# Splitting the last 1024 rows of a graph layer (dropout, 8192 x 8192 by 8192 x 64 matmul, residual, layer norm) into 896 and 128

## The chip, the cores and the metric

The kernel runs on one core of a Trainium2 chip. The metric is the device time of one execution in microseconds. In the profile's names PE is TensorE (PEld its weight loads), DVE VectorE, ACT ScalarE, POOL GpSimd and SP SyncE; a q behind a name means that engine's own queue.

## What is computed

```python
def _L0_gnn_ref(x, adj, u):
    keep = (u >= 0.1).astype(x.dtype)
    x_drop = x * keep / (1.0 - 0.1)
    return jnp.matmul(adj, x_drop)

x = _layernorm(x + _L0_gnn_ref(x, adj, L0_gnn_u), axis=-1)   # (x - mean) / sqrt(var + 1e-5)
```

All is fp32: x and u are 8192 x 64 (2.1 MB each), adj is 8192 x 8192 (268 MB), the output is 8192 x 64. Each element of adj is used once for 64 columns of output.

## The kernel before

x is held as 128 partitions by 64 chunks (CHUNKS) by 64 columns (D). dropped holds the dropped-out and scaled x. The product is made transposed: a chunk of dropped (128 x 64) is the stationary operand, adj's transposed columns stream past it, and acc in PSUM collects the 64 output columns of 512 rows on 64 partitions. TILES = 2 such column tiles, at partitions 0 and 64, work on different rows, so a block is 1024 rows (BLOCK) and there are 8 blocks. The host has laid adj out so that a piece, 8 chunks of a block, is one contiguous 4 MB; a block has 8 pieces.

SP loads the pieces in order into four slots of raw (lines 88 to 97); it waits, for each slot, until PE has multiplied the piece that was in it (multiplied). The very last piece is loaded in four parts of 4, 2, 1 and 1 chunks (FINE, line 99), each with its own semaphore. PE waits for each piece and multiplies it (multiply, line 109): 16 matmuls of 512 columns, each shown as two records since the data are fp32, 32 in all. After a block, ACT copies acc into sums (take_sums, line 144), PE turns it back with four 128-column matmuls against an identity (turn, line 117), and DVE adds x (line 170), makes statistics of eight groups of 64 columns (174, 178), adds epsilon (181); POOL raises to the power of -0.5 (201), DVE normalises (187), and ACT issues the store (store, line 148). ACT runs this in the order take_sums, store for each block; each engine's program is a list in order, and nothing is reordered between the waits. For all blocks but the last, this lies beside the next block's loads.

Of the kernel before, what the change touches and what calls it, by code (L numbers as in the profile page):

```python
# [16 lines left out]
LAST = BLOCKS * PIECES - 1  # L17
SLOTS = 4
ROUNDS = PIECES // SLOTS
FINE = [(0, 4), (4, 6), (6, 7), (7, 8)]  # L20
DMA = 16
# [5 lines left out]
def dropout_matmul_layernorm(nc, x, u, adj, out):  # L27
# [7 lines left out]
    with ExitStack() as ctx:  # L35
# [11 lines left out]
        raw = sbuf("raw", [P, SLOTS, PER_PIECE, BLOCK])  # L47
        eye = sbuf("eye", [P, P])
        sums = sbuf("sums", [P, BANK])
# [30 lines left out]
        out_stored = semaphore("out_stored")  # L80

# [144 lines left out]
```

## Time and profile before

| | |
|---|---|
| median of 3 runs | 657.78 us |
| lowest, highest | 657.72, 659.25 us |
| the profiled execution | 659.25 us |
| its span, first to last instruction | 657.5 us |
| PE busy | 492.7 us, 75% |
| DMA, mean over the span | 418 GB/s |

The profile was taken on the execution that took 659.25 us. Its page gives busy times by engine, a picture of the span in 40 slices, the chain of work that ended last and groups of instructions; the timeline and the stretches (windows) can be asked for any part of the span. Times in them count from the span's start.

### The profile page before, as it was taken

Reading aid. Unit: us, or ns where it says so; the run is one execution under the profiler, and the core shown is the slowest. Engines: PE = TensorE matmul, PEld = TensorE weight load, DVE = VectorE, ACT = ScalarE, POOL = GpSimd, SP = SyncE. Lnnn points to the kernel's source line nnn. Section 1 sums busy time; section 2 is a strip of 40 time slices with the busy share of each in tenths; the row PEclk is TensorE's granted clock in tenths of the full one; section 3 lists DMA queues with packets and bytes.
Section 4 is the critical chain, followed back from the end, with each engine's and each line's share of the span. In section 5 each row is a group of like instructions: output and inputs, shape, how many; then the busy total and the mean of one; then the engine's idle time right before and its main releaser. Section 6 shows DMA issues by size and latency. Waiting matters only on the chain.

```text
span 657.5 us, 4821 instructions
## 1 busy us (share of the span) xinstructions
PE 492.7 (75%) x2112; PEld 156.1 (24%) x2112; DVE 42.7 (6%) x210; ACT 6.0 (1%) x9; POOL 13.9 (2%) x15
## 2 busy tenths in 40 slices
PE   0587787786887697686796687877787688868784
PEld 0122222221222222222232222322232122312221
DVE  3000002000020001100020000200002000110002
ACT  0000000000000000000000000000000000000000
POOL 0000001000000000000000000000000000000000
PEclk9997989998989998998999988998999988999888
DMA  9999999999999999999999999999999999999980
GB/s 375 425 442 419 443 426 434 431 435 429 437 429 429 437 425 441 431 425 437 435 427 431 439 425 437 427 433 437 429 435 427 436 431 437 425 431 436 429 358 16
DMA packets 11094, 274.81 MB, mean 418 GB/s; under 512 B 1232, under 2 KB 1232, under 8 KB 2512
## 3 DMA queue, kind: packets, MB, share of 16 engines
q1 hardware_dynamic: 9936, 272.63, 96.5%
q10 hardware_dynamic: 1152, 2.10, 0.8%
q8 instruction: 4, 0.07, 0.0%
q14 instruction: 2, 0.02, 0.0%
HBM read 272.63 MB, written 2.10 MB: 418 GB/s over the span
## 4 chain that ended last, share of the span: by engine, by line
DMA 68%; PE 18%; issue 12%; DVE 1%; another core or an unknown queue 1%; SPq 0%; POOLq 0%; POOL 0%; ACT 0%; DVEq 0%
DMA raw<-adj_dram 68%; PE acc L109 17%; POOLq L35 0%; DVE normed L187 0%; POOL rstd L201 0%; PE turned L117 0%; DVE stats L174 0%; SPq L89 0%; SPq L94 0%; DVE rows L170 0%; DVE moments L178 0%; ACT sums L144 0%; SPq L87 0%; SPq L86 0%
## 5 line engine op out<-in xcount | busy, mean ns | idle before, releaser
L109 PE MATMUL acc<-raw,dropped 128*64 128x512 f32 x2048 | 483.6, 628 | 150.4 <-DMA raw<-adj_dram 150.4
L109 PEld LDWEIGHTS acc<-raw,dropped 128*64 128x64 f32 x2048 | 148.4, 144 | 479.7 <-issue 279.7
L170 DVE TENSOR_TENSOR rows<-turned,x_sb 128x512 f32<-128x512 f32 x8 | 5.5, 692 | 586.3 <-PE turned L117 586.3
L201 POOL TENSOR_TENSOR rstd<-var_eps,minus_half 128x8 f32<-128x8 f32 x8 | 13.1, 1640 | 638.5 <-DVE var_eps L181 638.5
L187 DVE TENSOR_SCALAR normed<-rows,moments,rstd 128x64 f32<-128x64 f32 x64 | 15.0, 310 | 14.1 <-POOL rstd L201 14.1
L117 PE MATMUL turned<-eye,sums 128*128 128x128 f32 x64 | 9.3, 288 | 5.5 <-ACT sums L144 5.5
L117 PEld LDWEIGHTS turned<-eye,sums 128*128 128x128 f32 x64 | 7.7, 191 | 12.5 <-ACT sums L144 12.5
L144 ACT COPY sums<-acc 128x512 f32<-128x512 f32 x8 | 4.7, 586 | 640.6 <-PE acc L109 640.6
L174 DVE BATCH_NORM_STATS2 stats<-rows 128x6 f32<-128x64 f32 x64 | 8.9, 212 | 0.3
L178 DVE BATCH_NORM_AGGREGATE moments<-stats 128x2 f32<-128x6 f32 x64 | 5.1, 153 | 0.3
L163 DVE TENSOR_TENSOR dropped<-dropped,x_sb 128x4096 f32<-128x4096 f32 x1 | 4.4, 4426 | 2.7 <-DMA x_sb<-x_dram 2.7
L159 DVE TENSOR_SCALAR dropped<-dropped 128x4096 f32<-128x4096 f32 x1 | 2.3, 2294 | 8.5 <-DMA dropped<-u_dram 8.5
L181 DVE TENSOR_SCALAR var_eps<-moments 128x8 f32<-128x8 f32 x8 | 1.4, 172 | 0.3
L144 ACT ACT_TABLE_LOAD x1 | 1.3, 1283 | 0.7 <-PEq L219 0.7
L196 POOL TENSOR_SCALAR_AFFINE_SELECT eye<-eye 128x128 f32<-128x128 f32 x1 | 0.3, 295 | 0.2 <-POOL eye L194 0.2
L194 POOL MEMSET eye<- 128x128 f32 x1 | 0.2, 205 | 0.0
L193 POOL MEMSET minus_half<- 128x8 f32 x1 | 0.1, 105 | 0.3 <-POOLq L219 0.3
L219 POOL MEMSET const-float32-0.0<- 128x1 f32 x1 | 0.1, 99 | 0.2 <-issue 0.2
L219 POOL MEMSET const-bfloat16-1.0<- 128x1 bf16 x1 | 0.1, 102 | 0.0
L219 POOL MEMSET const-uint8-127<- 128x1 uint8 x1 | 0.1, 102 | 0.0
L219 POOL MEMSET const-float32-1.0<- 128x1 f32 x1 | 0.1, 99 | 0.0
## 6 DMA issues: line engine op xcount, KB each, us to landing
raw<-adj_dram SPq DMA_DIRECT2D x63, 4096.0 KB, 31.5
dropped<-u_dram SPq DMA_DIRECT2D x1, 2048.0 KB, 7.7
x_sb<-x_dram SPq DMA_DIRECT2D x1, 2048.0 KB, 12.2
out_dram<-normed ACTq DMA_DIRECT2D x8, 256.0 KB, 14.3
raw<-adj_dram SPq DMA_DIRECT2D x1, 2048.0 KB, 26.9
raw<-adj_dram SPq DMA_DIRECT2D x1, 1024.0 KB, 29.0
raw<-adj_dram SPq DMA_DIRECT2D x2, 512.0 KB, 30.1
```

Of the source, the lines that this page charges most:

```text
L109: last = nc.tensor.matmul(acc[t * D:(t + 1) * D, :], dropped[:, c, :], raw[:, i % SLOTS, j, t * BANK:(t + 1) * BANK], start=(c == 0), stop ...
L117: last = nc.tensor.matmul(turned[:, i * TILES:(i + 1) * TILES, :], sums[:, i * P:(i + 1) * P], eye[:, :], start=True, stop=True)
L144: nc.scalar.copy(sums[:, :], acc[:, :]).then_inc(sums_ready, 1)
L159: nc.vector.tensor_scalar(dropped[:, :, :], dropped[:, :, :], P_DROP, 1.0 / (1.0 - P_DROP), ALU.is_ge, ALU.mult).then_inc(drop_scaled, 1)
L163: nc.vector.tensor_tensor(dropped[:, :, :], dropped[:, :, :], x_sb[:, :, :], ALU.mult).then_inc(x_dropped, 1)
L170: nc.vector.tensor_tensor(rows[:, :, :], turned[:, :, :], x_sb[:, b * GROUP:(b + 1) * GROUP, :], ALU.add).then_inc(rows_ready, 1)
L174: last = nc.vector.bn_stats(stats[:, i, :], rows[:, i, :])
L178: last = nc.vector.bn_aggr(moments[:, i, :], stats[:, i, :])
L181: nc.vector.tensor_scalar(var_eps[:, :], moments[:, :, 1], EPS, None, ALU.add).then_inc(var_ready, 1)
L187: last = nc.vector.tensor_scalar(normed[:, i, :], rows[:, i, :], moments[:, i, 0:1], rstd[:, i:i + 1], ALU.subtract, ALU.mult)
L201: nc.gpsimd.tensor_tensor(rstd[:, :], var_eps[:, :], minus_half[:, :], ALU.pow).then_inc(rstd_ready, 1)
L219: nc = bacc.Bacc("TRN2", target_bir_lowering=False, num_devices=1)
```

## The change

The first seven blocks stay as they are. The last 1024 rows become two parts.

NEXT is 896 rows: 448 in each column tile, all 64 chunks, in loads of 8, 8, 8, 8, 8, 8, 7, 5 and 4 chunks from an array of its own, adj_next, in which a partition's row holds all 64 chunks (224 KB). Its seven groups are turned (turn_next: three full matmuls, and two half ones for the group whose two halves lie in different tiles), normalised and stored as a block is.

FINAL is the last 128 rows. Both column tiles work on the same rows, tile 0 on chunks 0 to 31 and tile 1 on chunks 32 to 63: 32 pairs (PAIRS) of 128-column matmuls into final_acc, from loads of 10, 8, 6, 4, 2 and 2 pairs out of adj_final into slot 0. The turn of NEXT stands on PE behind the first of them, followed by a matmul that puts x of the last group into final_turned. At the end ACT copies final_acc to final_sums, one matmul against join (two identities, one above the other) turns it and adds the two halves onto x in final_turned, and DVE makes statistics and normalises straight from PSUM, one group wide; POOL has one more power. SP stores the last group. In ACT's program the copy stands behind NEXT's store.

The diff, cut to its core (declarations of the new tiles and semaphores, and edits of the normalising helper that only replace GROUP by groups, are left out):

```diff
@@ -6,25 +6,35 @@
 N = 8192
 D = 64
 CHUNKS = N // P
-BANK = 512
 TILES = 2
-TURNS = BANK // P
-BLOCK = TILES * BANK
-BLOCKS = N // BLOCK
-GROUP = TURNS * TILES
+DMA = 16
+
+
+WIDTH = 512
+GROUP = 8
+BLOCKS = 7
 PER_PIECE = 8
 PIECES = CHUNKS // PER_PIECE
-LAST = BLOCKS * PIECES - 1
 SLOTS = 4
 ROUNDS = PIECES // SLOTS
-FINE = [(0, 4), (4, 6), (6, 7), (7, 8)]
-DMA = 16
+ROW = PER_PIECE * TILES * WIDTH
+
+
+NEXT_WIDTH = 448
+NEXT_GROUP = 7
+NEXT = [(0, 0, 8), (1, 8, 16), (2, 16, 24), (3, 24, 32), (0, 32, 40), (1, 40, 48), (2, 48, 55), (3, 55, 60),
+        (3, 60, 64)]
+NEXT_ROUND = [s for s, _, _ in NEXT].index(0, 1)
+
+
+PAIRS = CHUNKS // TILES
+FINAL = [(0, 10), (10, 18), (18, 24), (24, 28), (28, 30), (30, 32)]
 
 P_DROP = 0.1
 EPS = 1e-5
 
 
-def dropout_matmul_layernorm(nc, x, u, adj, out):
+def dropout_matmul_layernorm(nc, x, u, adj, adj_next, adj_final, out):
     fp32 = mybir.dt.float32
     ALU = mybir.AluOpType
 
...
@@ -86,72 +112,111 @@
-                sp.dma_start(raw[:, s, :, :], adj[s]).then_inc(raw_loaded[s], DMA)
-            rounds = BLOCKS * ROUNDS
-            with sp.Fori(1, rounds - 1) as g:
+                sp.dma_start(raw[:, s, :], adj[s]).then_inc(raw_loaded[s], DMA)
+            with sp.Fori(1, BLOCKS * ROUNDS) as g:
                 for s in range(SLOTS):
                     sp.wait_ge(multiplied, (g - 1) * SLOTS + s + 1)
-                    sp.dma_start(raw[:, s, :, :], adj[g * SLOTS + s]).then_inc(raw_loaded[s], DMA)
-            for s in range(SLOTS - 1):
-                sp.wait_ge(multiplied, (rounds - 2) * SLOTS + s + 1)
-                sp.dma_start(raw[:, s, :, :], adj[(rounds - 1) * SLOTS + s]).then_inc(raw_loaded[s], DMA)
-            sp.wait_ge(multiplied, LAST - SLOTS + 1)
-            for f, (c0, c1) in enumerate(FINE):
-                sp.dma_start(raw[:, SLOTS - 1, c0:c1, :],
-                             adj[LAST][:, c0 * BLOCK:c1 * BLOCK]).then_inc(fine_loaded[f], DMA)
+                    sp.dma_start(raw[:, s, :], adj[g * SLOTS + s]).then_inc(raw_loaded[s], DMA)
+            chunk = TILES * NEXT_WIDTH
+            for n, (s, c0, c1) in enumerate(NEXT):
+
+                first_in_slot = c0 if s != SLOTS - 1 or n < NEXT_ROUND else NEXT[-2][1]
+                at = (c0 - first_in_slot) * chunk
+                sp.wait_ge(multiplied, BLOCKS * PIECES - SLOTS + min(n, len(NEXT) - 2) + 1)
+                sp.dma_start(raw[:, s, at:at + (c1 - c0) * chunk],
+                             adj_next[:, c0 * chunk:c1 * chunk]).then_inc(next_loaded[n], DMA)
+
+            sp.wait_ge(multiplied, BLOCKS * PIECES + NEXT_ROUND + 1)
+            for n, (q0, q1) in enumerate(FINAL):
+                sp.dma_start(raw[:, 0, q0 * TILES * P:q1 * TILES * P],
+                             adj_final[:, q0 * TILES * P:q1 * TILES * P]).then_inc(final_loaded[n], DMA)
+            sp.wait_ge(normed_ready, BLOCKS + 2)
+            sp.dma_start(out_dram[:, (CHUNKS - 1) * D:], final_normed[:, :]).then_inc(final_stored, DMA)
+            sp.wait_ge(final_stored, DMA)
...
-            def multiply(i, c0, c1):
-                for j in range(c0, c1):
-                    c = i * PER_PIECE + j
+            def multiply(s, at, c0, c1, width):
+                for c in range(c0, c1):
                     for t in range(TILES):
-                        last = nc.tensor.matmul(acc[t * D:(t + 1) * D, :], dropped[:, c, :],
-                                                raw[:, i % SLOTS, j, t * BANK:(t + 1) * BANK],
+                        start = at + ((c - c0) * TILES + t) * width
+                        last = nc.tensor.matmul(acc[t * D:(t + 1) * D, 0:width], dropped[:, c, :],
+                                                raw[:, s, start:start + width],
                                                 start=(c == 0), stop=(c == CHUNKS - 1))
                 return last
 
-            def turn(b):
-                pe.wait_ge(sums_ready, b + 1)
-                for i in range(TURNS):
-                    last = nc.tensor.matmul(turned[:, i * TILES:(i + 1) * TILES, :],
-                                            sums[:, i * P:(i + 1) * P], eye[:, :], start=True, stop=True)
-                last.then_inc(block_turned, 1)
+            def multiply_final(q0, q1):
+                for q in range(q0, q1):
+                    for t in range(TILES):
+                        start = (q * TILES + t) * P
+                        last = nc.tensor.matmul(final_acc[t * D:(t + 1) * D, 0:P], dropped[:, t * PAIRS + q, :],
+                                                raw[:, 0, start:start + P],
+                                                start=(q == 0), stop=(q == PAIRS - 1))
+                return last
+
+            def turn(groups):
+                for i in range(groups // TILES):
+                    last = nc.tensor.matmul(turned[:, i * TILES:(i + 1) * TILES, :], sums[:, i * P:(i + 1) * P],
+                                            eye[:, :], start=True, stop=True)
+                return last
+
+            def turn_next():
+                turn(NEXT_GROUP)
+
+                for t in range(TILES):
+                    last = nc.tensor.matmul(turned[t * D:(t + 1) * D, NEXT_GROUP - 1, :],
+                                            sums[:, NEXT_WIDTH - D:NEXT_WIDTH], eye[:, t * D:(t + 1) * D],
+                                            start=True, stop=True)
+                return last
...
-            with pe.Fori(0, BLOCKS - 1) as b:
+            pe.wait_ge(join_ready, 1)
+            with pe.Fori(0, BLOCKS) as b:
                 for i in range(PIECES):
                     pe.wait_ge(raw_loaded[i % SLOTS], (b * ROUNDS + i // SLOTS + 1) * DMA)
-                    multiply(i, 0, PER_PIECE).then_inc(multiplied, 1)
-                turn(b)
-            for i in range(PIECES - 1):
-                pe.wait_ge(raw_loaded[i % SLOTS], ((BLOCKS - 1) * ROUNDS + i // SLOTS + 1) * DMA)
-                multiply(i, 0, PER_PIECE).then_inc(multiplied, 1)
-            for f, (c0, c1) in enumerate(FINE):
-                pe.wait_ge(fine_loaded[f], DMA)
-                last = multiply(PIECES - 1, c0, c1)
-            last.then_inc(multiplied, 1)
-            turn(BLOCKS - 1)
+                    multiply(i % SLOTS, 0, i * PER_PIECE, (i + 1) * PER_PIECE, WIDTH).then_inc(multiplied, 1)
+                pe.wait_ge(sums_ready, b + 1)
+                turn(GROUP).then_inc(block_turned, 1)
+            for n, (s, c0, c1) in enumerate(NEXT):
+                pe.wait_ge(next_loaded[n], DMA)
+                at = (c0 - NEXT[-2][1]) * TILES * NEXT_WIDTH if n == len(NEXT) - 1 else 0
+                multiply(s, at, c0, c1, NEXT_WIDTH).then_inc(multiplied, 1)
+            for n, (q0, q1) in enumerate(FINAL):
+                if n == 1:
+                    pe.wait_ge(sums_ready, BLOCKS + 1)
+                    turn_next().then_inc(block_turned, 1)
+
+                    nc.tensor.matmul(final_turned[:, 0:D], eye[:, :], x_sb[:, CHUNKS - 1, :], start=True, stop=False)
+                pe.wait_ge(final_loaded[n], DMA)
+                last = multiply_final(q0, q1)
+            last.then_inc(final_multiplied, 1)
+            pe.wait_ge(final_sums_ready, 1)
+            nc.tensor.matmul(final_turned[:, 0:D], final_sums[:, :], join[:, :],
+                             start=False, stop=True).then_inc(final_done, 1)
...
-            def take_sums(b):
-                act.wait_ge(multiplied, (b + 1) * PIECES)
+            def take_sums(b, done, width):
+                act.wait_ge(multiplied, done)
                 if b:
 
                     act.wait_ge(rows_ready, b)
-                nc.scalar.copy(sums[:, :], acc[:, :]).then_inc(sums_ready, 1)
-
-            def store(b):
+                nc.scalar.copy(sums[:, 0:width], acc[:, 0:width]).then_inc(sums_ready, 1)
+
+            def store(b, groups):
                 act.wait_ge(normed_ready, b + 1)
-                act.dma_start(out_dram[:, b * GROUP * D:(b + 1) * GROUP * D],
-                              normed[:, :, :]).then_inc(out_stored, DMA)
+                act.dma_start(out_dram[:, b * GROUP * D:(b * GROUP + groups) * D],
+                              normed[:, 0:groups, :]).then_inc(out_stored, DMA)
 
             for b in range(BLOCKS):
-                take_sums(b)
-                store(b)
-            act.wait_ge(out_stored, BLOCKS * DMA)
+                take_sums(b, (b + 1) * PIECES, WIDTH)
+                store(b, GROUP)
+            take_sums(BLOCKS, BLOCKS * PIECES + len(NEXT), NEXT_WIDTH)
+            store(BLOCKS, NEXT_GROUP)
+            act.wait_ge(final_multiplied, 1)
+            nc.scalar.copy(final_sums[:, :], final_acc[:, 0:P]).then_inc(final_sums_ready, 1)
+            act.wait_ge(out_stored, (BLOCKS + 1) * DMA)
...
+            for b in range(BLOCKS):
+                normalise(b, GROUP)
+            normalise(BLOCKS, NEXT_GROUP)
+
+            dve.wait_ge(final_done, 1)
+            nc.vector.bn_stats(final_stats[:, :], final_turned[:, 0:D]).then_inc(stats_ready, 1)
+            dve.wait_ge(stats_ready, BLOCKS + 2)
+            nc.vector.bn_aggr(final_moments[:, :], final_stats[:, :]).then_inc(moments_ready, 1)
+            dve.wait_ge(moments_ready, BLOCKS + 2)
+            nc.vector.tensor_scalar(final_var[:, :], final_moments[:, 1:2], EPS, None, ALU.add).then_inc(var_ready, 1)
+            dve.wait_ge(rstd_ready, BLOCKS + 2)
+            nc.vector.tensor_scalar(final_normed[:, :], final_turned[:, 0:D], final_moments[:, 0:1],
+                                    final_rstd[:, 0:1], ALU.subtract, ALU.mult).then_inc(normed_ready, 1)
...
-            nc.gpsimd.memset(eye[:, :], 0.0).then_inc(eye_zeroed, 1)
-            pool.wait_ge(eye_zeroed, 1)
+            nc.gpsimd.memset(eye[:, :], 0.0).then_inc(squares_zeroed, 1)
+            nc.gpsimd.memset(join[:, :], 0.0).then_inc(squares_zeroed, 1)
+            pool.wait_ge(squares_zeroed, 2)
             nc.gpsimd.affine_select(out=eye[:, :], in_=eye[:, :], compare_op=ALU.not_equal, fill=1.0,
                                     base=0, pattern=[[-1, P]], channel_multiplier=1).then_inc(eye_ready, 1)
+            nc.gpsimd.affine_select(out=join[:, :], in_=join[:, :], compare_op=ALU.not_equal, fill=1.0,
+                                    base=0, pattern=[[-1, D]], channel_multiplier=1).then_inc(join_half, 1)
+            pool.wait_ge(join_half, 1)
+            nc.gpsimd.affine_select(out=join[:, :], in_=join[:, :], compare_op=ALU.not_equal, fill=1.0,
+                                    base=-D, pattern=[[-1, D]], channel_multiplier=1).then_inc(join_ready, 1)
...
+            pool.wait_ge(var_ready, BLOCKS + 2)
+            nc.gpsimd.tensor_tensor(final_rstd[:, :], final_var[:, :], minus_half[:, 0:1],
+                                    ALU.pow).then_inc(rstd_ready, 1)
...
-    pieces = by_row.transpose(1, 5, 4, 6, 3, 2, 0)
+    by_group = np.asarray(adj).reshape(P, CHUNKS, P, CHUNKS).transpose(1, 2, 3, 0)
+
+    full = by_group[:BLOCKS * GROUP].reshape(BLOCKS, GROUP // TILES, TILES, P, PIECES, PER_PIECE, P)
+    full = full.transpose(0, 4, 3, 5, 2, 1, 6)
+
+    first = CHUNKS - 1 - NEXT_GROUP
+    whole = by_group[first:CHUNKS - 2].reshape(NEXT_GROUP // TILES, TILES, P, CHUNKS, P).transpose(2, 3, 1, 0, 4)
+    halves = by_group[CHUNKS - 2].reshape(P, CHUNKS, TILES, P // TILES)
+    nxt = np.concatenate([whole.reshape(P, CHUNKS, TILES, -1), halves], axis=3)
+
+    final = by_group[CHUNKS - 1].reshape(P, TILES, PAIRS, P).transpose(0, 2, 1, 3)
```

## Rows read from the trace of the kernel before

**Rows 1.** The page: span, DMA's busy tenths in 40 slices, HBM bytes

```profile
span 657.5 us, 4821 instructions
...
DMA  9999999999999999999999999999999999999980
...
HBM read 272.63 MB, written 2.10 MB: 418 GB/s over the span
```

**Rows 2.** A stretch of the middle: busy time of each engine, clock, DMA share, GB/s

```profile
core 0: us, PE busy (x) PEld busy (x) DVE busy (x) ACT busy (x) POOL busy (x), PEclk, DMA share, GB/s
100.00:200.00 100.00, 78.14 (x336) 25.16 (x336) 8.99 (x52) 0.86 (x2) 3.29 (x2) 0.95 1.00 432
```

**Rows 3.** The page's chain that ended last, by line

```profile
DMA raw<-adj_dram 68%; PE acc L109 17%; POOLq L35 0%; DVE normed L187 0%; POOL rstd L201 0%; PE turned L117 0%; DVE stats L174 0%; SPq L89 0%; SPq L94 0%; DVE rows L170 0%; DVE moments L178 0%; ACT sums L144 0%; SPq L87 0%; SPq L86 0%
```

**Rows 4.** Timeline of PE and its weight loads near the end: start, length, instructions [idle before]

```profile
601.91 0.20 PEld L109 LDWEIGHTS acc<-raw,dropped 128*64 128x64 f32 x4 [3.49 <-DMA raw<-adj_dram]
...
621.34 7.09 PE L109 MATMUL acc<-raw,dropped 128*64 128x512 f32 x32 [1.03 <-DMA raw<-adj_dram]
631.05 15.65 PE L109 MATMUL acc<-raw,dropped 128*64 128x512 f32 x64 [2.62 <-DMA raw<-adj_dram]
```

**Rows 5.** Stretches near the end (columns as in group 2)

```profile
632.00:634.00 2.00, 2.00 (x8) 0.69 (x6) 0.00 (x0) 0.00 (x0) 0.00 (x0) 0.50 0.94 397
...
636.00:638.00 2.00, 2.00 (x12) 0.62 (x10) 0.00 (x0) 0.00 (x0) 0.00 (x0) 1.00 1.00 408
...
640.00:641.00 1.00, 1.00 (x8) 0.33 (x6) 0.00 (x0) 0.00 (x0) 0.00 (x0) 1.00 0.04 16
```

**Rows 6.** Timeline behind the last adj matmul, all engines

```profile
646.75 0.59 ACT L144 COPY sums<-acc 128x512 f32<-128x512 f32 x1 [76.58 <-PE acc L109]
647.39 0.97 PEld L117 LDWEIGHTS turned<-eye,sums 128*128 128x128 f32 x8 [1.57 <-ACT sums L144]
647.39 1.16 PE L117 MATMUL turned<-eye,sums 128*128 128x128 f32 x8 [0.69 <-ACT sums L144]
648.65 0.69 DVE L170 TENSOR_TENSOR rows<-turned,x_sb 128x512 f32<-128x512 f32 x1 [70.82 <-PE turned L117]
649.38 1.11 DVE L174 BATCH_NORM_STATS2 stats<-rows 128x6 f32<-128x64 f32 x8
650.53 0.64 DVE L178 BATCH_NORM_AGGREGATE moments<-stats 128x2 f32<-128x6 f32 x8
651.20 0.17 DVE L181 TENSOR_SCALAR var_eps<-moments 128x8 f32<-128x8 f32 x1
651.45 1.64 POOL L201 TENSOR_TENSOR rstd<-var_eps,minus_half 128x8 f32<-128x8 f32 x1 [75.53 <-DVE var_eps L181]
653.13 1.88 DVE L187 TENSOR_SCALAR normed<-rows,moments,rstd 128x64 f32<-128x64 f32 x8 [1.75 <-POOL rstd L201]
655.03 0.34 ACTq L148 DMA_DIRECT2D out_dram<-normed  x1
```

**Rows 7.** DMA issues of the last 57 us: size, us from issue to landing

```profile
out_dram<-normed ACTq DMA_DIRECT2D x1, 256.0 KB, 2.0
```

**Rows 8.** Durations of single instructions: ns min/median/max, then busy us, mean ns

```profile
L109 PEld LDWEIGHTS acc<-raw,dropped x2048: 132/137/232, 23.1 to 645.7; 128*64 128x64 f32 x187
L109 PE MATMUL acc<-raw,dropped x2048: 592/592/1116, 23.1 to 646.1; 128*64 128x512 f32 x187
...
L174 DVE BATCH_NORM_STATS2 stats<-rows 128x6 f32<-128x64 f32 x64 | 8.9, 212 | 0.3
L117 PEld LDWEIGHTS turned<-eye,sums 128*128 128x128 f32 x64 | 7.7, 191 | 12.5 <-ACT sums L144 12.5
L178 DVE BATCH_NORM_AGGREGATE moments<-stats 128x2 f32<-128x6 f32 x64 | 5.1, 153 | 0.3
```

**Rows 9.** Timeline of SP's queue near the end

```profile
609.04 1.75 SPq L100 DMA_DIRECT2D raw<-adj_dram  x4
```

**Rows 10.** The page's group of POOL's select

```profile
L196 POOL TENSOR_SCALAR_AFFINE_SELECT eye<-eye 128x128 f32<-128x128 f32 x1 | 0.3, 295 | 0.2 <-POOL eye L194 0.2
```

More of the change, by code:

```diff
@@ L46, in dropout_matmul_layernorm @@
         dropped = sbuf("dropped", [P, CHUNKS, D])
-        raw = sbuf("raw", [P, SLOTS, PER_PIECE, BLOCK])
+        raw = sbuf("raw", [P, SLOTS, ROW])
         eye = sbuf("eye", [P, P])
-        sums = sbuf("sums", [P, BANK])
+        join = sbuf("join", [P, D])
+        sums = sbuf("sums", [P, WIDTH])
+        final_sums = sbuf("final_sums", [P, P])
         rows = sbuf("rows", [P, GROUP, D])
@@ L56, in dropout_matmul_layernorm @@
         normed = sbuf("normed", [P, GROUP, D])
-        acc = psum("acc", [P, BANK])
+        final_stats = sbuf("final_stats", [P, 6])
+        final_moments = sbuf("final_moments", [P, 2])
+        final_var = sbuf("final_var", [P, 1])
+        final_rstd = sbuf("final_rstd", [P, 1])
+        final_normed = sbuf("final_normed", [P, D])
+        acc = psum("acc", [P, WIDTH])
         turned = psum("turned", [P, GROUP, D])
+        final_acc = psum("final_acc", [P, WIDTH])
+        final_turned = psum("final_turned", [P, WIDTH])
         x_loaded = semaphore("x_loaded")
@@ L64, in dropout_matmul_layernorm @@
         raw_loaded = [semaphore(f"raw_loaded{s}") for s in range(SLOTS)]
-        fine_loaded = [semaphore(f"fine_loaded{f}") for f in range(len(FINE))]
+        next_loaded = [semaphore(f"next_loaded{n}") for n in range(len(NEXT))]
+        final_loaded = [semaphore(f"final_loaded{n}") for n in range(len(FINAL))]
         drop_scaled = semaphore("drop_scaled")
         x_dropped = semaphore("x_dropped")
-        eye_zeroed = semaphore("eye_zeroed")
+        squares_zeroed = semaphore("squares_zeroed")
+        join_half = semaphore("join_half")
         eye_ready = semaphore("eye_ready")
+        join_ready = semaphore("join_ready")
         minus_half_ready = semaphore("minus_half_ready")
         multiplied = semaphore("multiplied")
+        final_multiplied = semaphore("final_multiplied")
         sums_ready = semaphore("sums_ready")
+        final_sums_ready = semaphore("final_sums_ready")
         block_turned = semaphore("block_turned")
+        final_done = semaphore("final_done")
         rows_ready = semaphore("rows_ready")
@@ L164, in _, with normalise @@
                                     ALU.mult).then_inc(x_dropped, 1)
-            for b in range(BLOCKS):
+            def normalise(b, groups):
                 if b:
@@ L169, in _ @@
                 dve.wait_ge(block_turned, b + 1)
-                nc.vector.tensor_tensor(rows[:, :, :], turned[:, :, :], x_sb[:, b * GROUP:(b + 1) * GROUP, :],
-                                        ALU.add).then_inc(rows_ready, 1)
+                nc.vector.tensor_tensor(rows[:, 0:groups, :], turned[:, 0:groups, :],
+                                        x_sb[:, b * GROUP:b * GROUP + groups, :], ALU.add).then_inc(rows_ready, 1)
                 dve.wait_ge(rows_ready, b + 1)
-                for i in range(GROUP):
+                for i in range(groups):
                     last = nc.vector.bn_stats(stats[:, i, :], rows[:, i, :])
@@ L176, in _ @@
                 dve.wait_ge(stats_ready, b + 1)
-                for i in range(GROUP):
+                for i in range(groups):
                     last = nc.vector.bn_aggr(moments[:, i, :], stats[:, i, :])
@@ L185, in _ @@
                     dve.wait_ge(out_stored, b * DMA)
-                for i in range(GROUP):
+                for i in range(groups):
                     last = nc.vector.tensor_scalar(normed[:, i, :], rows[:, i, :], moments[:, i, 0:1],
@@ L216 @@
         "u_dram": np.ascontiguousarray(L0_gnn_u),
-        "adj_dram": np.ascontiguousarray(pieces).reshape(BLOCKS * PIECES, P, PER_PIECE * BLOCK),
+        "adj_dram": np.ascontiguousarray(full).reshape(BLOCKS * PIECES, P, ROW),
+        "adj_next_dram": np.ascontiguousarray(nxt).reshape(P, CHUNKS * TILES * NEXT_WIDTH),
+        "adj_final_dram": np.ascontiguousarray(final).reshape(P, CHUNKS * P),
     }
```

9 lines of the change are left out of this document (5 added, 4 removed).

## The prediction, made before the changed kernel was run

> **What bounds the kernel now.** I read the page first. The DMA row is at nine tenths in every slice but the last two, and adj makes up 268 of the 272.63 MB read [rows 1]. A stretch of the middle confirms it: 432 GB/s with a DMA share of 1.00, while PE is busy for 78 us of 100 [rows 2]. The chain of waits says the same: 68% of the span lies on loads of raw, 17% on the matmuls of line 109 [rows 3]. So up to the last load the time is bytes over bandwidth, and neither the bytes nor their order up to there are changed. The reader should therefore look only at what comes after the stream.
>
> The end of the timeline [rows 4] tells that part. A 4 MB piece lands each 9.71 us (621.34, 631.05) and takes PE 7.09 us, so PE idles 2.6 us before the next. Piece 62 lands at 631.05. Piece 63, loaded in four parts, is then worked off with no further wait: 64 records in one run to 646.70. The stream moves 408 GB/s until 638 and only 16 after 640 [rows 5]: 16 KB, and the last byte is in by about 640.4. PE is thus 6.3 us behind the last byte: piece 62 cannot start before 631.05, and two pieces are 14 us of matmuls while the DMA needs 9.4. A stretch of half clock (granted clock 0.50 behind 632, which is 1.2 GHz, after PE's idle 2.6 us, and 1.00 again by 636) added 1.7 us, for 15.65 stands against 13.95 at full clock [rows 4, 5]. Behind it the serial chain of a whole block [rows 6]: copy 0.59, turns 1.16, rows 0.69, statistics 1.11 and 0.64, variance 0.17, power on POOL 1.64, normalising 1.88, store. The store is issued at 655.03, lands 2.0 us later [rows 7], and the span ends 0.47 us after that. So 17.1 us lie behind the last byte: 6.3 of PE, 10.8 of chain and store.
>
> **The change part by part.** Bytes are the same: 448 columns in each tile are 7/8 of a block, and the final 128 rows are the last eighth, 4 MB. NEXT therefore ends at the byte where piece 62 ended, and I let its last load land at 631.05 too.
>
> *Matmuls of NEXT.* A piece of 8 chunks takes 7.09 us, of which 0.23 is the last record's tail (592 ns long against a pace of some 0.43 for two records, one of each tile) [rows 4, 8]: 0.857 us per chunk, 0.75 with 448 columns. The loads of 7, 5 and 4 chunks land at 1.06 us per chunk (9.71 x 7/8 / 8), at 621.5, 626.8 and 631.05, and PE takes 5.25, 3.75 and 3.0: it is done at 626.8, 630.6 and 634.05. The 2.6 us gap before 631.05 nearly vanishes, and with it, I assume, the half clock.
>
> *Final matmuls.* 32 pairs of chunks, each one 128-column matmul per tile, four records. The row of the turns is the nearest: 8 records of 128 columns in 1.16 us, and eight loads of weights in 0.97 us, of 191 ns each, hence a pace of (0.97 - 0.19) / 7 = 0.111 us [rows 6, 8]; I use 0.112. In line 109 the two tiles run side by side, as two records in 0.43 us against a 592 ns record show. I take 0.224 us per pair of chunks, twice 0.112; the low end is a quarter of 0.857, 0.214; the high end is two tiles that do not overlap when matmuls are this short, 0.45. The row for the low end is nearest, since the weight loads (137 ns for both tiles together) lie under streaming even now.
>
> *Loads of FINAL.* The parts of 10, 8, 6, 4, 2, 2 pairs of chunks share 9.4 us (631.05 to 640.44), so they land at about 634.0, 636.3, 638.1, 639.3, 639.9 and 640.4. SP issues six instead of four parts at 0.44 us each [rows 9]; it may once NEXT's fifth load is multiplied, about 611.6, with 19 us of stream still queued. Nothing is queued behind them but the final store, so they cost nothing. Their rows of 2 to 10 KB are covered by the fine loads of before, of which the last were 4 KB per partition: the queue still moved 408 GB/s from 636 to 638 [rows 5].
>
> *First final part, then the turn.* PE starts at 634.05 (data at 634.0), 10 x 0.224 later it is 636.3. The sums copy (0.59 or less) has ended by 635.0, hidden behind this. Seven groups are turned with 3 full and 2 half matmuls, 10 records: 1.12 us, to 637.4, and the last result 0.16 later (what 1.16 us leave beyond eight paces and the first one's start of 0.1); I add 0.1 for the change from half-width to full-width tiles, which no row shows alone (0 to 0.3). The matmul that puts x into final_turned is 2 records, 0.2. Then 22 pairs x 0.224 = 4.93: PE ends at 642.7 and its result is there at 642.9. All data are there by 640.4, so PE is 2.5 instead of 6.3 us behind.
>
> *NEXT's chain*, now beside those matmuls: rows start at 637.85 (the wait after turns is 0.11 [rows 6]), 0.62, statistics 0.97, aggregates 0.56, variance 0.17, power 1.64 (at most), normalising 1.65, with 0.25 us of gaps as before: 643.75. Here is the wait that takes over. ACT's store of these seven groups stands in its queue ahead of the final copy, and the copy can't start until normed_ready has come and the DMA is issued, 0.34 us [rows 6]: 644.15, which is 1.25 us after PE is ready. From there on this, not PE and not the DMA, sets the end.
>
> *Final chain.* Copy of 128 columns: between 0.15 (a quarter of 586 ns) and 0.59; 0.3, since the DVE rows of 64 and 6 elements (212 and 153 ns) show a large fixed part [rows 8]. Join: two records; 1.16 less seven paces leaves 0.38 for a first record and its load, so 0.50 for two with the wait (0.3 to 0.6). One bn_stats 0.21, one bn_aggr 0.15, variance 0.17, with 0.2 of waits. Power over 128x1 instead of 128x8: 1.64 at most [rows 6], 0.2 if only elements count (an eighth); a select of 16 times as many elements takes 0.3 [rows 10], so elements alone don't make the price. I take 1.0, near the middle, as no row is near. One normalising 0.31. Wait and store: 2.0 to landing, as for 256 KB (1.5 at the low end, as an eighth of the bytes may land sooner), then 0.47. Sum from 644.15: 0.30 + 0.50 + 0.10 + 0.21 + 0.04 + 0.15 + 0.04 + 0.17 + 0.07 + 1.0 + 0.04 + 0.31 + 0.03 + 2.0 + 0.47 = 5.43, span 649.6 against 657.5: 7.9 us less.
>
> *At the start* POOL gets one more memset and two more selects (up to 0.3 us each [rows 10]) before PE may begin; PE's first data come at 23.1 [rows 8], so they are free. At full blocks nothing changes but names.
>
> **The rivals.**
> *PE is slow on short matmuls.* At 0.45 us per pair of chunks the first part ends 2.3 us later and the rest 4.9 more: PE ends at 650.1, the final copy starts there instead of 644.15, 5.9 later, and the time is 655.8. For it: no row has two tiles at 128 columns, with four instructions per 0.22 us. Against: the turns keep 0.11 per record, and after a wait four weight loads start within 0.20 us [rows 4]. It decides from 0.28 us per pair of chunks on; below that ACT's wait covers PE's end and only the ten pairs ahead of the turn count, so at 0.274 (137 ns of weight load not covered) it costs 0.5.
> The Trainium skill (TensorE: Matmul & The Clock Gate, Back-to-back issue gap) gives 81 ns per bf16 load-and-matmul pair at 128 columns where streaming alone would be 56. By that excess of 25 ns for each of four records a pair of chunks would take 0.32 and the time near 651.9; the turns' 0.112 against 0.107 of two streamings of 128 columns (256 columns at 2.4 GHz) disagrees with it.
>
> *Half clock in the tail.* One such stretch cost 1.7 us in before, as told above. If it falls between 631 and 642, the path is 1.7 longer at most: 651.6. For it: NEXT's loads of 8 chunks leave gaps of 2.5 us, like those before. Against: from 621.5 on PE has no gap over half a microsecond.
>
> *The stream slows (the slower side).* Until now a load was one contiguous 4 MB with 32 KB per partition. NEXT's rows lie 224 KB apart in HBM. 29.4 MB pass in 68 us at 432 GB/s; each per cent of rate lost is 0.7 us on the path, with nothing to hide it. The gain is used up at 387 GB/s, and at 370 the loads take 79.4 us: 11.4 more, less 7.9, time 661.3. For it: no row has this pitch. Against: the four fine loads, 16 to 4 KB out of rows that lie 32 KB apart and so not contiguous either, ran at 408 GB/s until the queue emptied [rows 5].
> [...]
>
> *Nothing is won.* Slow short matmuls and half clock together give 657.5, no change.
>
> **How the numbers follow.** The forecast is the sum: the median of 657.78 less 7.9 is 649.9. (The profiled execution was 659.25 with a span of 657.5; by that one it would be 651.35, and I go by the median, as two of three runs are within 0.1 of it.) Its own bounds: power -0.8 and +0.64, copy -0.15 and +0.29, join and drains -0.25 and +0.35, store -0.5, PE's pace up to +0.5: 648.2 to 651.7. Chances: forecast 0.66, slow short matmuls 0.12 (655.8), half clock 0.11 (651.6), no change 0.05, slower stream 0.06 (661 and above). Range 648.2 to 656.0, which leaves out the last two. A measurement here can tell 0.3%, 2.0 us, from no change: faster 0.89, same 0.05, slower 0.06.
>
> **What would show it.** In the profile after: the rate stays 432 GB/s after 572; the last NEXT matmul ends near 634.2 and the first turn starts near 636.3; final matmuls advance 0.22 us per pair of chunks and end near 642.9; ACT's final copy follows its DMA issue at about 644.15 with PE done before; POOL's last power is 0.2 to 1.64 us; the last store is issued near 647.1. Wrong would be: any stall of PE on the final loads, granted clock 0.50 after 631, or a last NEXT landing much after 631.

## The result, and the profile after

The changed kernel takes 650.32 us (median of 4 runs, 650.16 to 650.56) against 657.75 (4 runs, 657.67 to 659.25): ratio 0.9882, interval 0.9865 to 0.9899, 7.4 us less. The profiled execution took 650.56 us with a span of 648.7. In every run below for which both are known the time is the span plus 1.7 to 1.9 us, so spans and times are compared with that offset.

The page, first: span, DMA's busy tenths, bytes. They answer to [rows 1].

```profile
span 648.7 us, 5089 instructions
...
DMA  9999999999999999999999999999999999999994
...
HBM read 272.63 MB, written 2.10 MB: 424 GB/s over the span
```

The bytes are the same and the DMA row is full to the last slice but one; what is gone is idle DMA at the end. The chain by line, which answers to [rows 3], has the new array's loads in it and the matmuls of acc at 21% instead of 17%; of the final part's own work only names with 0%:

```profile
DMA raw<-adj_dram 68%; PE acc L143 21%; DMA raw<-adj_next_dram 9%; PE final_acc L152 0%; POOL rstd L287 0%; SPq L115 0%; DVE stats L239 0%; SPq L119 0%; PE turned L159 0%; DVE rows L235 0%; POOLq L45 0%; DVE moments L243 0%; SPq L113 0%; SPq L112 0%; DVE final_normed L267 0%
```

Stretches (busy time of PE, PEld, DVE, ACT, POOL, then granted clock, DMA share, GB/s), which answer to [rows 2] and [rows 5]:

```profile
core 0: us, PE busy (x) PEld busy (x) DVE busy (x) ACT busy (x) POOL busy (x), PEclk, DMA share, GB/s
100.00:200.00 100.00, 76.37 (x336) 24.77 (x336) 8.98 (x52) 0.78 (x2) 3.31 (x2) 0.97 1.00 432
...
632.00:634.00 2.00, 2.00 (x14) 0.81 (x12) 0.00 (x0) 0.00 (x0) 0.00 (x0) 1.00 1.00 418
...
640.00:641.00 1.00, 1.00 (x22) 1.00 (x20) 0.69 (x8) 0.00 (x0) 0.20 (x1) 1.00 0.12 45
```

The rate is as before, and the stream is nearly over in the stretch from 640, as it was. PE's granted clock is 1.00 from 620 until its last matmul at 645; it falls only after 646, when PE has nothing left to do. PE's timeline in the tail, which answers to [rows 4]:

```profile
614.43 20.32 PE L143 MATMUL acc<-raw,dropped 128*64 128x448 f32 x96 [2.27 <-DMA raw<-adj_next_dram]
634.61 2.40 PE L152 MATMUL final_acc<-raw,dropped 128*64 128x128 f32 x40
636.94 0.94 PE L159 MATMUL turned<-eye,sums 128*128 128x128 f32 x6
...
638.44 5.02 PE L152 MATMUL final_acc<-raw,dropped 128*64 128x128 f32 x88
```

And what the other engines do, which answers to [rows 6]:

```profile
634.79 0.53 ACT L205 COPY sums<-acc 128x448 f32<-128x448 f32 x1 [64.71 <-PE acc L143]
...
638.26 0.63 DVE L235 TENSOR_TENSOR rows<-turned,x_sb 128x448 f32<-128x448 f32 x1 [60.51 <-PE turned L167]
...
640.80 1.48 POOL L287 TENSOR_TENSOR rstd<-var_eps,minus_half 128x7 f32<-128x7 f32 x1 [64.96 <-DVE var_eps L246]
642.32 1.65 DVE L252 TENSOR_SCALAR normed<-rows,moments,rstd 128x64 f32<-128x64 f32 x7 [1.60 <-POOL rstd L287]
644.00 0.34 ACTq L209 DMA_DIRECT2D out_dram<-normed  x1
644.38 0.27 ACT L218 COPY final_sums<-final_acc 128x128 f32<-128x128 f32 x1 [9.05 <-DVE normed L252]
...
645.17 0.23 DVE L261 BATCH_NORM_STATS2 final_stats<-final_turned 128x6 f32<-128x64 f32 x1 [1.20 <-PE final_turned L195]
645.44 0.18 DVE L263 BATCH_NORM_AGGREGATE final_moments<-final_stats 128x2 f32<-128x6 f32 x1
645.65 0.15 DVE L265 TENSOR_SCALAR final_var<-final_moments 128x1 f32<-128x1 f32 x1
645.88 0.55 POOL L290 TENSOR_TENSOR final_rstd<-final_var,minus_half 128x1 f32<-128x1 f32 x1 [3.60 <-DVE final_var L265]
646.47 0.34 DVE L267 TENSOR_SCALAR final_normed<-final_turned,final_moments,final_rstd 128x64 f32<-128x64 f32 x1 [0.67 <-POOL final_rstd L290]
646.84 0.34 SPq L134 DMA_DIRECT2D out_dram<-final_normed  x1
```

The last two stores (issue, size, us to landing), as in [rows 7]:

```profile
out_dram<-normed ACTq DMA_DIRECT2D x1, 224.0 KB, 1.9
out_dram<-final_normed SPq DMA_DIRECT2D x1, 32.0 KB, 1.5
```

The loads of FINAL: duration of the issues in ns (min/median/max) with their first and last start, then the time from issue to landing:

```profile
L131 SPq DMA_DIRECT2D raw<-adj_final_dram x6: 328/432/433, 612.2 to 614.5; - x6
...
DMA to landing us min/median/max: 22.4/26.3/27.0
```

The reader sees: PE multiplies NEXT until the first final part at 634.61, turns at 636.94, and ends FINAL at 643.46 (638.44 + 5.02). The last load has landed at 641.5 (614.5 + 27.0), so PE is 2.0 us behind it. In the profile of before the last load landed at 640.9 and PE was 5.8 us behind, 1.7 of them by the stretch of half clock. NEXT's whole chain runs beside FINAL's matmuls and ends at 643.97. ACT issues its store at 644.00 and only then, at 644.38, copies FINAL's sums, although PE had been done for 0.9 us. Behind the copy lies a chain of one group, 4.3 us to the end of the span, where [rows 6] and the store had 10.7.

### The profile page after: what moved, and what is told of

The parts are those of the page before. It is cut to its first block, busy times and chain, and to the rows that moved or that the text cites. A ratio compares the mean times of both kernels' runs of the same rounds, so it can differ in the third digit from the quotient of the medians.

```text
span 648.7 us, 5089 instructions
## 1 busy us (share of the span) xinstructions
PE 503.8 (78%) x2246; PEld 165.9 (26%) x2246; DVE 43.1 (7%) x211; ACT 6.2 (1%) x10; POOL 14.8 (2%) x19
## 4 chain that ended last, share of the span: by engine, by line
DMA 76%; PE 21%; issue 1%; SPq 1%; DVE 0%; POOL 0%; POOLq 0%; DVEq 0%
DMA raw<-adj_dram 68%; PE acc L143 21%; DMA raw<-adj_next_dram 9%; PE final_acc L152 0%; POOL rstd L287 0%; SPq L115 0%; DVE stats L239 0%; SPq L119 0%; PE turned L159 0%; DVE rows L235 0%; POOLq L45 0%; DVE moments L243 0%; SPq L113 0%; SPq L112 0%; DVE final_normed L267 0%
## 5 line engine op out<-in xcount | busy, mean ns | idle before, releaser
L143 PE MATMUL acc<-raw,dropped 128*64 128x512 f32 (+1 forms) x2048 | 486.6, 632 | 135.3 <-DMA raw<-adj_dram 124.5
L143 PEld LDWEIGHTS acc<-raw,dropped 128*64 128x64 f32 x2048 | 150.6, 146 | 465.6 <-issue 281.0
L235 DVE TENSOR_TENSOR rows<-turned,x_sb 128x512 f32<-128x512 f32 (+1 forms) x8 | 5.5, 683 | 575.7 <-PE turned L159 515.2
L287 POOL TENSOR_TENSOR rstd<-var_eps,minus_half 128x8 f32<-128x8 f32 (+1 forms) x8 | 13.0, 1623 | 627.1 <-DVE var_eps L246 627.1
L205 ACT COPY sums<-acc 128x512 f32<-128x512 f32 (+1 forms) x8 | 4.6, 579 | 628.7 <-PE acc L143 628.7
L152 PE MATMUL final_acc<-raw,dropped 128*64 128x128 f32 x128 | 7.4, 274 | 0.0
L152 PEld LDWEIGHTS final_acc<-raw,dropped 128*64 128x64 f32 x128 | 6.9, 137 | 0.7 <-DMA raw<-adj_final_dram 0.6
L246 DVE TENSOR_SCALAR var_eps<-moments 128x8 f32<-128x8 f32 (+1 forms) x8 | 1.4, 171 | 0.3
```

The source lines that it names most:

```text
L143: last = nc.tensor.matmul(acc[t * D:(t + 1) * D, 0:width], dropped[:, c, :], raw[:, s, start:start + width], start=(c == 0), stop=(c == CH ...
L152: last = nc.tensor.matmul(final_acc[t * D:(t + 1) * D, 0:P], dropped[:, t * PAIRS + q, :], raw[:, 0, start:start + P], start=(q == 0), sto ...
L205: nc.scalar.copy(sums[:, 0:width], acc[:, 0:width]).then_inc(sums_ready, 1)
L235: nc.vector.tensor_tensor(rows[:, 0:groups, :], turned[:, 0:groups, :], x_sb[:, b * GROUP:b * GROUP + groups, :], ALU.add).then_inc(rows_r ...
L246: nc.vector.tensor_scalar(var_eps[:, 0:groups], moments[:, 0:groups, 1], EPS, None, ALU.add).then_inc(var_ready, 1)
L287: nc.gpsimd.tensor_tensor(rstd[:, 0:groups], var_eps[:, 0:groups], minus_half[:, 0:groups], ALU.pow).then_inc(rstd_ready, 1)
```

## The experiments

Each edit is against the changed kernel unless it says otherwise. The kernel before ran beside them on the same chip: 657.76 us (12 runs) beside the first four, 657.74 (13 runs) beside the others.

**ACT's copy ahead of its store.**

```diff
-            store(BLOCKS, NEXT_GROUP)
             act.wait_ge(final_multiplied, 1)
             nc.scalar.copy(final_sums[:, :], final_acc[:, 0:P]).then_inc(final_sums_ready, 1)
+            store(BLOCKS, NEXT_GROUP)
```

> The changed kernel with ACT's final copy placed ahead of NEXT's store instead of behind it. Theory: the store's wait for normed_ready and its issue hold the copy back; in the profile of the changed kernel the copy starts at 644.38 while the last final matmul is done at 643.46, so the copy should start at 643.5 and the time fall by 0.85 us, to 649.5. Rival: PE and DVE set the end and the store's place is harmless (DVE is busy with NEXT until 643.97): no change, 650.3.

Measured: 649.49 us (4 runs, 649.37 to 649.74), ratio to before 0.9867 (0.985 to 0.9885). Its timeline, all engines:

```profile
642.09 1.65 DVE L252 TENSOR_SCALAR normed<-rows,moments,rstd 128x64 f32<-128x64 f32 x7 [1.59 <-POOL rstd L287]
643.27 0.27 ACT L217 COPY final_sums<-final_acc 128x128 f32<-128x128 f32 x1 [8.18 <-PE final_acc L152]
...
643.77 0.34 ACTq L209 DMA_DIRECT2D out_dram<-normed  x1
...
645.74 0.34 SPq L134 DMA_DIRECT2D out_dram<-final_normed  x1
```

The copy starts at 643.27, when PE is ready (638.20 + 5.02 = 643.22), while DVE is still normalising NEXT; the store follows at 643.77 and loses nothing. In the contiguous kernel below, which has the old order and whose last NEXT load landed at the same time (631.3), the copy starts at 644.13. The wait that the prediction had named as the one that takes over is shown, and its price, 0.8 to 0.9 us, with it. The four runs of this kernel and the four of the changed one don't overlap.

**Finer loads alone**, in the kernel before: the last two pieces in seven loads, with a turn and a chain of 1024 rows as ever.

```diff
-FINE = [(0, 4), (4, 6), (6, 7), (7, 8)]
+FINE = [(2, 0, 4), (2, 4, 8), (3, 0, 3), (3, 3, 5), (3, 5, 6), (3, 6, 7), (3, 7, 8)]
...
+            for f, (s, c0, c1) in enumerate(FINE):
+                if c0 == 0:
+                    sp.wait_ge(multiplied, LAST - SLOTS - (SLOTS - 1 - s) + 1)
+                sp.dma_start(raw[:, s, c0:c1, :],
+                             adj[LAST - (SLOTS - 1 - s)][:, c0 * BLOCK:c1 * BLOCK]).then_inc(fine_loaded[f], DMA)
```

> The kernel before, with only finer loads: piece 62 in 4 and 4 chunks, piece 63 in 3, 2, 1, 1, 1; block of 1024 rows and chain unchanged. Theory: PE was 6.3 us behind the stream because it got piece 62 whole; with 0.857 us per chunk it would work (4) 631.05 to 634.5, (3) to 637.2, (2) to 638.9, then one by one to 641.5, so the last matmul ends near 641.7 instead of 646.7, the chain of 10.8 us follows, and the time is 652.7: two thirds of the gain without any split. Rival: the gain comes from the narrow last group, and finer loads bring under 1 us: 656.8 or more.

Measured: 654.86 us (4 runs, 654.78 to 654.93), ratio 0.9948 (0.993 to 0.9966), 2.9 us less than before, where 5.1 were expected. Its timeline:

```profile
621.58 0.20 PEld L110 LDWEIGHTS acc<-raw,dropped 128*64 128x64 f32 x4 [3.50 <-DMA raw<-adj_dram]
642.45 0.58 ACT L146 COPY sums<-acc 128x512 f32<-128x512 f32 x1 [72.08 <-PE acc L110]
...
650.73 0.34 ACTq L150 DMA_DIRECT2D out_dram<-normed  x1
```

The chain behind the matmuls is the old one (642.45 to 650.73, 8.3 us, as from 646.75 to 655.03 in [rows 6]). The matmuls end at 642.40, not 641.7: PE got piece 61 whole at 621.58 and has worked without a pause since, 24 chunks at 0.857 us, which I had not counted. The larger part of the miss is the point of comparison: 646.7 was the end in the profile of before; the last experiment below has it at 645.1, with the time that most runs have. From there 2.7 us were to be had, and 2.9 were measured.

**The split alone**: NEXT in eights, FINAL in one load of 4 MB, the turn ahead of its matmuls.

```diff
+        (1, 40, 48), (2, 48, 56), (3, 56, 64)]
...
+FINAL = [(0, 32)]
...
-                if n == 1:
+                if n == 0:
```

> The changed kernel without shrinking loads: NEXT in eight loads of 8 chunks, FINAL in one load of 4 MB, the turn ahead of its matmuls. Theory: the last NEXT load is worked off from 631.5 to 637.7, FINAL's data are there at 640.5 and its 32 pairs take 7.1 us, so PE ends near 647.7 instead of 643.46, NEXT's chain is long done, the final chain of 4.3 us follows: 3.3 us later than the changed kernel, time 653.7. Rival: the split alone brings all of the gain, 650.3; other rival: without shrinking loads nothing is gained, 657.7.

Measured: 654.55 us (4 runs, 654.27 to 655.92), ratio 0.9942 (0.9924 to 0.996). PE's and ACT's rows of its timeline, then three stretches of it (columns as above):

```profile
640.93 8.84 PE L150 MATMUL final_acc<-raw,dropped 128*64 128x128 f32 x128 [1.26 <-DMA raw<-adj_final_dram]
...
649.82 0.27 ACT L215 COPY final_sums<-final_acc 128x128 f32<-128x128 f32 x1 [11.76 <-PE final_acc L150]
```

```profile
640.00:642.00 2.00, 1.07 (x10) 1.07 (x12) 1.78 (x16) 0.00 (x0) 0.04 (x1) 0.72 0.00 0
642.00:644.00 2.00, 2.00 (x24) 2.00 (x22) 0.52 (x3) 0.00 (x0) 1.44 (x1) 0.50 0.00 0
644.00:648.00 4.00, 4.00 (x74) 4.00 (x72) 1.13 (x6) 0.00 (x0) 0.00 (x0) 0.96 0.18 59
```

FINAL's data come at 640.93, PE has idled 1.26 us before them and then has 32 pairs to do with nothing left to hide them. This profile is of the run of 655.92: a stretch of half clock lies on the final matmuls (0.50 from 642 to 644), so that they take 8.84 us. The other three runs are between 654.27 and 654.60. With 7.2 us for the 32 pairs at full clock (2.40 for the first ten of the changed kernel, 0.218 for each further one) the copy would start at 648.2 instead of the changed kernel's 644.38, 3.8 later, and 4.2 were measured. The theory's 653.7 is missed by 0.85: the one large load lands at 640.9, 0.4 later than assumed; the rest is open. Neither rival holds: each half of the change brings some 3 us (2.9 and 3.2), and both together 7.4. The two 3s are made differently. Finer loads move PE's end forward by 2.7 us and leave the chain. The split shortens what follows PE's end from 10.7 to 4.3 us, but as FINAL comes in one load, PE ends some 3 us later (648.1 against 645.1), and this eats half of that.

**One column tile for FINAL.** The join then runs over 64 partitions.

```diff
-nc.tensor.matmul(final_acc[t * D:(t + 1) * D, 0:P], dropped[:, t * PAIRS + q, :],
+nc.tensor.matmul(final_acc[0:D, 0:P], dropped[:, t * PAIRS + q, :],
```

> The changed kernel with all 64 chunks of FINAL in column tile 0, so that its matmuls cannot run two at a time, and the join over 64 partitions. Theory: a pair of chunks takes 0.45 us instead of 0.222, the ten ahead of the turn 2.2 us more and the other 22 another 4.9; PE ends at 650.6 instead of 643.46, past ACT's wait (which moves to 646.6), and the copy starts 6.2 us later: time 656.5, almost all of the gain lost. Rival: the two tiles hardly overlap when matmuls are short, or the loads of FINAL set the pace: under 2 us lost, 652.3 or less.

Measured: 656.42 us (9 runs, 656.29 to 656.51), ratio 0.9974 (0.9964 to 0.9984). PE's timeline:

```profile
634.53 4.58 PE L152 MATMUL final_acc<-raw,dropped 128*64 128x128 f32 x40
...
640.54 9.82 PE L152 MATMUL final_acc<-raw,dropped 128*64 128x128 f32 x88
```

40 records in 4.58 us and 88 in 9.82, where the changed kernel has 2.40 and 5.02. The 12 pairs between the two counts take 5.24 us, 0.437 each, against 2.62, 0.218 each: the two tiles do run side by side even at 128 columns, and this is worth 6.1 of the 7.4 us. It disproves the first rival of the prediction by building it.

**The pitch of NEXT's rows.** One kernel lays each load of NEXT out contiguous, the other puts its rows 512 KB apart instead of 224.

```diff
+                             adj_next[P * c0 * chunk:P * c1 * chunk].rearrange(
+                                 "(p e) -> p e", p=P)).then_inc(next_loaded[n], DMA)
```

```diff
+        "adj_next_dram": np.pad(np.ascontiguousarray(nxt).reshape(P, CHUNKS * TILES * NEXT_WIDTH),
+                                ((0, 0), (0, 131072 - CHUNKS * TILES * NEXT_WIDTH))),
```

> The changed kernel with each load of NEXT contiguous in HBM instead of rows 224 KB apart. In the profile of the changed kernel the last NEXT load landed at 631.52, 0.47 us later than piece 62 did before. Theory: the pitch costs nothing and the 0.47 us are the larger number of transfers or chance: landing between 631.2 and 631.6, time 650.3 within 0.3. Rival: the pitch slows the stream by 0.7%: landing at 631.05, time 649.9 or less.

> The changed kernel with the rows of NEXT 512 KB apart instead of 224 KB. Rival of the prediction (slower side), taken to its strongest form: if a pitch that is a large power of two halves the rate, the 29.4 MB take 142 instead of 68 us and the time is near 724. Theory: with loads that write SBUF and 28 KB per row the rate holds, 432 GB/s and 650.3.

Measured: contiguous 650.26 us (4 runs, 650.21 to 650.31), ratio 0.9883 (0.9867 to 0.9899); 512 KB pitch 650.41 (2 runs), ratio 0.9886 (0.9866 to 0.9905). The last NEXT load of the contiguous kernel, from PE's timeline, and of the 512 KB one:

```profile
631.27 3.23 PE L144 MATMUL acc<-raw,dropped 128*64 128x448 f32 x16 [0.31 <-DMA raw<-adj_next_dram]
```

```profile
631.38 3.23 PE L143 MATMUL acc<-raw,dropped 128*64 128x448 f32 x16 [0.31 <-DMA raw<-adj_next_dram]
```

A stretch of the changed kernel, and the same of the 512 KB one:

```profile
570.00:600.00 30.00, 23.88 (x118) 9.01 (x120) 4.49 (x26) 0.09 (x1) 1.64 (x1) 0.94 1.00 430
```

```profile
570.00:600.00 30.00, 23.84 (x120) 8.88 (x121) 4.48 (x26) 0.00 (x0) 1.64 (x1) 0.94 1.00 430
```

The rates are equal, and the last load lands at 631.27 and 631.38, against 631.52 in the changed kernel and 631.29 in the copy-first one, whose loads are those of the changed kernel. So landing varies by 0.2 us from one profile to the next, whatever the pitch, and the slower-side rival has nothing behind it at 224 KB nor at 512: a halved rate, as supposed above, would have given some 724 us. The Trainium skill (DMA: Bandwidth & Descriptors, Latency and other measured facts) gives 207 GB/s for copies between HBM tensors at a row pitch of 512 KiB, beside 214 as the full rate, so 3% less. By that, as an estimate, the 68 us of NEXT's loads would be 2.3 us longer and the time some 652.6. Here, with loads into SBUF of 28 KB per row, the kernel took 650.41 and the trace shows 430 GB/s over these 30 us, and the measurement decides.

**Finer still**, on top of copy-first: the x matmul goes ahead of NEXT, NEXT's last load and FINAL's first are split, and the turn stands behind the first 4 pairs.

```diff
+        (3, 60, 62), (3, 62, 64)]
...
+FINAL = [(0, 4), (4, 10), (10, 18), (18, 24), (24, 28), (28, 30), (30, 32)]
```

> The copy-first kernel (649.49) with three more edits: NEXT's last load of 4 chunks split into 2 and 2, FINAL's first load of 10 pairs into 4 and 6 with the turn behind the 4, and the matmul that puts x into final_turned moved ahead of NEXT. Theory: PE's lag behind the stream is what is left. PE had a gap of 0.9 us at 630.6 that a load of 2 chunks fills, and 0.25 us of the x matmul leave the tail: the last final matmul ends at 642.1 instead of 643.2, time 648.4. Rival: the first final load or the added transfers gate PE instead, or DVE, busy with NEXT until 643.7 minus the earlier turn, does: 649.2 or more.

Measured: 648.45 us (4 runs, 648.42 to 648.57), ratio 0.9856 (0.984 to 0.9873). PE's timeline up to FINAL, then the tail of all engines:

```profile
614.33 19.84 PE L142 MATMUL acc<-raw,dropped 128*64 128x448 f32 x96 [2.28 <-DMA raw<-adj_next_dram]
```

```profile
634.98 0.94 PE L158 MATMUL turned<-eye,sums 128*128 128x128 f32 x6
...
636.01 6.30 PE L151 MATMUL final_acc<-raw,dropped 128*64 128x128 f32 x112
...
640.35 1.65 DVE L250 TENSOR_SCALAR normed<-rows,moments,rstd 128x64 f32<-128x64 f32 x7 [1.59 <-POOL rstd L285]
642.36 0.27 ACT L215 COPY final_sums<-final_acc 128x128 f32<-128x128 f32 x1 [7.60 <-PE final_acc L151]
642.36 0.34 ACTq L207 DMA_DIRECT2D out_dram<-normed  x1
...
644.82 0.34 SPq L133 DMA_DIRECT2D out_dram<-final_normed  x1
```

The loads of FINAL, as above:

```profile
L130 SPq DMA_DIRECT2D raw<-adj_final_dram x7: 327/433/8283, 612.1 to 622.7; - x7
...
DMA to landing us min/median/max: 18.8/24.2/26.5
```

PE now runs from 614.33 without a gap between results. The gap that it had before NEXT's last load was 0.3 us (0.31 in the contiguous and the 512 KB kernel above), not 0.9: the 0.9 in the expectation is the idle time of the weight loads. The first turn is at 634.98 (636.94 in the changed kernel), FINAL ends at 642.31, DVE is done with NEXT at 642.00, just ahead of the copy at 642.36. The three edits were made together, so the 1.0 us isn't divided among them by a run; in the traces FINAL's first record starts 0.4 us earlier than in copy-first (634.01, 634.38), and from there to PE's end it is 8.3 us instead of 8.8, with the x matmul's 0.4 gone from it. One of SP's seven issues for FINAL took 8.28 us instead of 0.43, for a reason that no run shows; the last went out at 622.7 and landed at 641.5 (622.7 + 18.8), as the last one does in the changed kernel. This is the fastest kernel of the study, 1.9 us under the changed one. PE ends 0.8 us behind the last landing, and its work on the last two pairs is some 0.6 of it (0.218 each and the end of the last record), so PE's lag is nearly used up; what is left is the final chain of 4.3 us.

**The kernel before, once more.**

> The kernel before, unchanged, profiled anew. Its times fall into two groups, 657.6 to 657.9 and 659.2 to 659.4, and the profile of before was of the second. Theory: the 1.6 us between them are the half-clock stretch that lay in its tail (15.65 us for the last 64 records instead of 13.95): a profile of the first group has granted clock 1.00 from 631 to 645, its last adj matmul ends near 645.0 and its span is 655.9. Rival: the groups differ elsewhere (in the loads or the first blocks), and the last 64 records take 15.6 us in both.

Measured: 657.95 us (10 runs, 657.45 to 659.31), ratio to the other runs of before 1.0008 (0.9997 to 1.0018). The profiled run is one of 657.66 with a span of 655.9. PE's timeline, which answers to [rows 4]:

```profile
602.02 8.78 PE L109 MATMUL acc<-raw,dropped 128*64 128x512 f32 x32 [2.66 <-DMA raw<-adj_dram]
611.74 7.09 PE L109 MATMUL acc<-raw,dropped 128*64 128x512 f32 x32 [0.93 <-DMA raw<-adj_dram]
621.44 7.09 PE L109 MATMUL acc<-raw,dropped 128*64 128x512 f32 x32 [2.62 <-DMA raw<-adj_dram]
631.16 13.95 PE L109 MATMUL acc<-raw,dropped 128*64 128x512 f32 x64 [2.63 <-DMA raw<-adj_dram]
```

The last 64 records take 13.95 us here, 15.65 in [rows 4]; the half-clock stretch lies on the piece at 602.02 (8.78 us), where the next wait for data swallows it. That is the whole difference between the two profiled runs (1.70 us, less 0.11 by which the load came later here; the spans are 1.6 apart). That it is so in the other runs of the two groups is inferred from their times alone. Of these 10 runs four are near 659.3, and seven of the 25 that ran beside the experiments. None of the 27 runs of the changed kernel and of the experiments built on it with the shrinking loads (the split-only kernel is apart) stands 1.6 us above the others. Why is not shown. From 622 until its last final matmul PE idles at most 0.3 us at a time in them, and the stretches of half clock behind 560 us in all ten profiles followed an idle of 2.2 to 3.0 us, or the 1.26 of the split-only kernel. But idles of 2.6 us, and those of 1.2 at 621.6 in three of the kernels, were followed by none, so the idle time alone does not decide, and it was not varied by itself.

## Why the prediction was right

The forecast was 649.9 us and 650.32 was measured. The mechanism came out step by step, but the closeness of the number is partly luck, two errors that offset each other.

- *What bounds it.* The stream up to 631: right. The rate is the same, and the last NEXT load lands at 631.52, with 631.05 assumed.
- *NEXT's matmuls.* 634.05 forecast for their end; the first final record starts at 634.61. The landing is 0.47 of it; the other 0.09 is a wait for FINAL's first load, which landed at 634.6 (612.2 + 22.4), not 634.0.
- *Loads of FINAL.* The sum let them land between 634.0 and 640.4; they landed between 634.6 and 641.5. The "last byte" of the stretches is not yet the landing that PE waits for: in the kernel before it came at 640.9 too. Apart from the 0.09 it cost nothing, as PE was later still.
- *Short matmuls.* 0.224 us per pair of chunks taken, 0.214 the low end. Measured: (5.02 - 2.40) / 12 = 0.218, between the two. Two column tiles with four records overlap as fully at 128 columns as at 512, as the one-tile kernel shows from the other side (0.437 per pair). The excess of 25 ns per load-and-matmul that the Trainium skill's 81 ns (TensorE: Matmul & The Clock Gate, Back-to-back issue gap) would give is not there in these fp32 records: with one tile they follow each other by 0.109 us, 0.002 more than two streamings of 128 columns.
- *First turn* 636.94 (forecast 636.3), *PE's end* 643.46 (642.9), *NEXT's chain* 643.97 (643.75), *ACT's final copy* 644.38 (644.15). The first two are off by 0.6, most of it the 0.47 of the landing; the last two by 0.2, since from the first turn to DVE's rows it took 1.3 us instead of 1.55, and the power over seven columns 1.48 instead of 1.64. The sum itself is not clean here: its written terms give 637.78 for the rows and 643.98 for the copy, where the text carries 637.85 and 644.15. The wait behind ACT's store was named as what sets the end, and moving the copy gave 0.8 us back.
- *Final chain.* The one mis-sized stretch of the path: 5.43 forecast from copy to end, 4.32 measured. The power over one element took 0.55, not 1.0; the store of 32 KB landed after 1.5, not 2.0 us, and 0.36 instead of 0.47 lay behind it. Copy 0.27, statistics 0.23 and 0.18, variance 0.15, normalising 0.34 are within 0.04 of the terms. So the forecast span of 649.6 is 0.9 too long.
- *From span to median.* This step failed. I subtracted 7.9 us, taken against a profile with 1.7 us of half clock in its tail, from a median of runs that mostly don't have it. The kernel before has 655.9 as its usual span, and the sum should have said 6.3 less against the median, so 651.5, or 651.35 by the profiled run, as the text also noted. The 1.1 us of chain that the sum had too much brought it back; that is luck.

The rivals: slow short matmuls are disproved (the one-tile kernel shows what it would have cost), a slower stream is disproved at pitches of 224 and 512 KB, half clock in the tail did not come in the changed kernel, though the split-only kernel shows that it can behind a split, at 1.3 to 1.7 us. The signs named for being wrong stayed away but for the 0.09 us of PE's wait.

## What to carry to other kernels

In a kernel bound by a stream, what follows the last byte is two things in a row: how far the computing engine lags, which is set by the size of the last several loads and not of the last one alone (in the finer-loads kernel PE, at 71% of the stream's time per chunk, had not caught up two pieces after the last whole one), and the serial chain, which is set by how much output hangs on the last byte. Shrinking only one of them gave 3 us, both 7.4, because a narrow last part in one load makes the lag longer. When a stage is split in two, look in each engine's list for the first half's store or wait standing ahead of the second half's first step; and before a saving is subtracted from a median, see whether the profile shows a run of that median.

## What the hardware showed that was not expected

- The power on POOL took 0.55 us for 128x1, 1.48 for 128x7 and 1.64 for 128x8: some 0.16 us per column on top of 0.39.
- Rows 512 KB apart in HBM were loaded at the same 430 GB/s as contiguous ones.
- A single half-clock stretch makes the 1.6 us between the two profiled runs of the kernel before, and so probably its two groups of times. It costs nothing when it falls on a piece that is followed by a wait for data, as at 602.02 there and at 614.43 in the changed kernel (granted clock 0.50 from 616 to 618).
